# A Mamba block with a ternary feed-forward layer: both layer norms from one set of statistics, small operations moved to GpSimd, weight quantised before the loop, 80 instead of 88 C products on GpSimd

## The reference

```
def mamba_dir(h, ...):                      # once forward, once on the flipped sequence
    x, z = h @ W_in.T                       # 256 channels each
    x = silu(conv4(x) + conv_b)
    dt, Bm, Cm = x @ Wx.T                   # 64 + 16 + 16
    dt = softplus(dt @ Wdt.T + bdt)
    hc = exp(dt * A) * hc + dt * x * Bm     # over 1024 steps, 256 channels x 16 states
    y  = sum_n(hc * Cm) + x * D
    return (y * silu(z)) @ W_out.T
def layernorm(x): return (x - mean(x)) / sqrt(var(x) + 1e-5)

x  = layernorm(h + mamba_fwd(h) + flip(mamba_rev(flip(h))))
# feed-forward
xn = (x - mean(x)) * rsqrt(var(x) + 1e-3) * ln_gamma + ln_beta
w_q = clip(round(w / (mean|w| + 1e-5)), -1, 1);  gamma = max|xn| over everything
y  = clip(xn * 128 / gamma) @ w_q * (gamma * mean|w| / 128)
out = layernorm(x + y)
```

## Time and profile before

| | |
|---|---|
| time, three runs | 985.17, 985.58, 991.32 us (median 985.58) |
| the profiled execution | 983.27 us, of which the span of the core is 981.4 us |
| granted TensorE clock, mean | 0.819 of full speed |
| DVE busy | 883.9 us, 90% of the span, 998 instructions |
| POOL busy | 860.1 us, 88%, 392 instructions |
| ACT / PE busy | 594.0 us, 61% / 647.7 us, 66% |
| the loop | about 42 to 928 us; before it the set-up, behind it the tail |

### The profile page before, as it was taken

One profiled execution on the slowest core, in us unless ns is written; L12 is line 12 of the kernel. 1 busy time (PEld: TensorE's weight loads), 2 busy tenths in 40 slices (PEclk: granted clock), 3 DMA queues, 4 the chain that ended last, 5 costly groups with the idle time before them and its releaser, 6 DMA issues. The chain is left out here.

```text
span 981.4 us, 8254 instructions
## 1 busy us (share of the span) xinstructions
PE 647.7 (66%) x2076; PEld 216.6 (22%) x2076; DVE 883.9 (90%) x998; ACT 594.0 (61%) x966; POOL 860.1 (88%) x392
## 2 busy tenths in 40 slices
PE   6667666868676767858576767757576677655432
PEld 3222122213122222213122121213122121111032
DVE  2388999999999999999999999999999999999945
ACT  2576556665765656665766666665665756663415
POOL 0399999999999999999999999999999999999502
PEclk9977888779798798789699798889699887577656
DMA  2767347564454747564454746564544746640102
GB/s 58 196 174 140 120 86 161 121 133 107 92 141 96 170 86 152 129 135 102 89 144 96 172 86 142 139 129 103 91 123 97 175 86 137 144 87 12 50 26 85
DMA packets 46735, 113.11 MB, mean 115 GB/s; under 512 B 7136, under 2 KB 20448, under 8 KB 46560
## 3 DMA queue, kind: packets, MB, share of 16 engines
q1 hardware_dynamic: 46688, 112.59, 51.4%
HBM read 40.48 MB, written 4.98 MB: 46 GB/s over the span
## 5 line engine op out<-in xcount | busy, mean ns | idle before, releaser
L428 POOL TENSOR_TENSOR dbx<-step_rep,bc_rep 128x1024 f32<-128x1024 f32 x256 | 598.2, 2364 | 16.7 <-DMA step_rep<-step 12.0
L623 ACT ACTIVATE da_ps<-step_rep,neg_a 128x512 f32<-128x512 f32 x512 | 349.7, 689 | 276.0 <-DVE hs L882 270.4
L882 DVE TENSOR_TENSOR_SCAN hs<-da_ps,dbx 128x512 f32<-128x512 f32 x256 | 297.1, 1210 | 30.2 <-POOL dbx L428 14.4
L882 DVE TENSOR_TENSOR_SCAN hs<-da_ps,carry,dbx 128x512 f32<-128x512 f32 x256 | 312.9, 1270 | 12.2 <-ACT da_ps L623 11.8
L1131 PE MATMUL y_ps<-ch,stack 128*32 128x512 f32 x1024 | 173.5, 755 | 188.4 <-DVE ch L770 121.3
L438 POOL TENSOR_TENSOR ch<-hs,bc_rep 128x1024 f32<-128x1024 f32 x88 | 207.7, 2361 | 27.5 <-issue 16.6
L770 DVE TENSOR_TENSOR ch<-hs,c_ps 128x1024 f32<-128x1024 f32 x168 | 201.4, 1199 | 0.0
L1122 PE MATMUL c_ps<-x_dbl,select 128*128 128x512 f32 x256 | 175.5, 774 | 0.0
L1077 PE MATMUL pre<-h_t,w_conv 128*128 128x512 f32 x256 | 119.4, 610 | 6.9 <-ACT xs L529 5.4
L1131 PEld LDWEIGHTS y_ps<-ch,stack 128*32 128x32 f32 x1024 | 24.4, 119 | 300.4 <-issue 173.8
L1122 PEld LDWEIGHTS c_ps<-x_dbl,select 128*128 128x128 f32 x256 | 46.2, 225 | 140.6 <-issue 127.7
(11 more groups left out here) (127 smaller groups left out, 500.5 us busy)
## 6 DMA issues: line engine op xcount, KB each, us to landing
step_rep<-step SPq DMA_DIRECT2D x128, 512.0 KB, 8.3
bc_rep<-bc_rows SPq DMA_DIRECT2D x64, 512.0 KB, 5.6
h_in<-in_L_attn_hidden_states SPq DMA_DIRECT2D x4, 512.0 KB, 8.8
h_res<-in_L_attn_hidden_states SPq DMA_DIRECT2D x4, 512.0 KB, 9.1
out<-hs SPq DMA_DIRECT2D x4, 512.0 KB, 3.2
x_rows<-xn SPq DMA_DIRECT2D x7, 256.0 KB, 7.9
dbx<-x_rows SPq DMA_DIRECT2D x1, 1536.0 KB, 6.6
bc_rows<-x_dbl SPq DMA_DIRECT2D x16, 64.0 KB
```

The source lines that it names most:

```text
L428: nc.gpsimd.tensor_tensor(dbx[:, n % RING], dtx_rep[:, r], b_rep[:, s % 2, k, :].unsqueeze(1).to_broadcast([P, 2, CHUNK]), ALU.mult).then_ ...
L623: nc.scalar.activation(da_ps[:, half % DA_BANKS, :], dt_rep[:, r, e, :], ACT.Exp, scale=neg_a[:, half_of(unit), 2 * (unit % 2) + e, g, k:k ...
L882: nc.vector.tensor_tensor_scan(in_scan_order(hs[:, n % RING, e, :], s), in_scan_order(da_ps[:, (2 * n + e) % DA_BANKS, :], s), in_scan_ord ...
```

## The change

Variance under a second layer norm follows from the first: if v is the variance of `resid`, x has variance v/(v+eps1), and the two norms together multiply by (v(1+eps2) + eps1*eps2) ** -0.5. So both come from one mean and one variance.

- DVE keeps `resid`, four `bn_stats` and four `bn_aggr` (into `mv`). The second set of statistics, both additions of eps and both biases leave DVE.
- POOL gets `both_norms` at n = 6 in place of `inverse_deviation` at n = 6 and at n = 9: three small `tensor_scalar` (128x4), one power of 128x8, one product 128x8, with a wait on its own result ahead of the last two.
- ACT at n = 8: `normalise`, now `resid` -> `xhat`, a new tile that PE transposes; at n = 9: `keep_x1`, `resid` -> `xn`, with the other scale. In the tail `keep_x1` comes after `norm_out`.
- `residual` on DVE waits until ACT has read the `resid` before (`xn_ready`, `x1_ready`), not for PE.
- `quantise_weight` moves into `copy_weights`, after the first copy, ahead of a wait for PE.
- `POOL_C` has five units in every group, (1, 4, 8, 11, 13): 80 C products on POOL, 176 on DVE.

```
-CLOSING = {"save": 3, "start sum": 3, "gate": 2, "output": 4, "residual": 5, "mean1": 6, "deviation1": 6,
-           "bias1": 7, "scale1": 8, "statistics2": 8, "mean2": 9, "deviation2": 9, 
-           "bias2": 10, "scale2": 11, "transpose": 12, "affine": 14, "largest": 14}
+CLOSING = {"save": 3, "start sum": 3, "gate": 2, "output": 4, "residual": 5, "mean": 6, "deviation": 6,
+           "scale": 8, "keep": 9, "transpose": 12, "affine": 14, "largest": 14}
-POOL_C = ((1, 3, 6, 8, 11, 13), (1, 4, 8, 11, 13)) * (NG // 2)
+POOL_C = ((1, 4, 8, 11, 13),) * NG
...
-            def inverse_deviation(e, mv, mv_ready, rstd, rstd_ready, eps):
-
-                pool.wait_ge(mv_ready, 2 * (e + 1))
-                nc.gpsimd.tensor_tensor(rstd[:], mv[:, :, 1], half[:, 0:TT], ALU.pow).then_inc(rstd_ready, 1)
+            def both_norms(e):
+
+                pool.wait_ge(mv_ready, e + 1)
+                if e:
+                    pool.wait_ge(x1_ready, TT * e)
+                    pool.wait_ge(xn_ready, TT * e)
+                nc.gpsimd.tensor_scalar(spread_of[:, 0, :], mv[:, :, 1], LN1_EPS, None, ALU.add).then_inc(spread_ready, 1)
+                nc.gpsimd.tensor_scalar(spread_of[:, 1, :], mv[:, :, 1], 1.0 + LN2_EPS, LN1_EPS * LN2_EPS,
+                                        ALU.mult, ALU.add).then_inc(spread_ready, 1)
+                nc.gpsimd.tensor_scalar(neg_mean[:], mv[:, :, 0], -1.0, None, ALU.mult).then_inc(spread_ready, 1)
+                pool.wait_ge(spread_ready, 3 * (e + 1))
+                nc.gpsimd.tensor_tensor(rstd[:].rearrange("p l t -> p (l t)"), spread_of[:].rearrange("p l t -> p (l t)"),
+                                        half[:, 0:2 * TT], ALU.pow).then_inc(rstd_ready, 1)
+                pool.wait_ge(rstd_ready, e + 1)
+                nc.gpsimd.tensor_tensor(bias[:], rstd[:], neg_mean[:].unsqueeze(1).to_broadcast([P, 2, TT]),
+                                        ALU.mult).then_inc(bias_ready, 1)
...
             def normalise(b_e, h_e):
                 e = 2 * b_e + h_e
-                act.wait_ge(bias1_ready, e + 1)
+                act.wait_ge(bias_ready, e + 1)
+                if e:
+                    act.wait_ge(xn_ps, e)
+                for j in range(TT):
+                    nc.scalar.activation(xhat[:, j, :], resid[:, j, :], ACT.Identity, scale=rstd[:, 1, j:j + 1],
+                                         bias=bias[:, 1, j:j + 1]).then_inc(xn_ready, 1)
+            def keep_x1(b_e, h_e):
...
+                    nc.scalar.activation(xn[:, j, :], resid[:, j, :], ACT.Identity, scale=rstd[:, 0, j:j + 1],
+                                         bias=bias[:, 0, j:j + 1]).then_inc(x1_ready, 1)
...
             def copy_weights():
                 dve.wait_ge(weights_ps, 1)
                 nc.vector.tensor_copy(w_z_t[:], c_ps[:, 0, 0:INNER]).then_inc(weights_sb, 1)
+                quantise_weight()
                 dve.wait_ge(weights_ps, 4)
...
+            def residual(b, h_e):
...
+                dve.wait_ge(o_ps, e + 1)
+                if e:
+                    dve.wait_ge(xn_ready, TT * e)
+                    dve.wait_ge(x1_ready, TT * e)
...
+            def mean(b, h_e):
+
+                e = 2 * b + h_e
+                dve.wait_ge(stats_ready, TT * (e + 1))
+                if e:
+                    dve.wait_ge(bias_ready, e)
                 for j in range(TT):
                     ins = nc.vector.bn_aggr(mv[:, j, :], stats[:, j, :])
                 ins.then_inc(mv_ready, 1)
...
-                        if first and s == 1 and n == 4:
-                            quantise_weight()
```

More of the change, by code:

```diff
@@ L164, in build @@
         stats = sb("stats", [P, TT, 6])
[L165 to L170, removed]
+        mv = sb("mv", [P, TT, 2])
+        spread_of = sb("spread_of", [P, 2, TT])
+        neg_mean = sb("neg_mean", [P, TT])
+        rstd = sb("rstd", [P, 2, TT])
+        bias = sb("bias", [P, 2, TT])
+        xhat = sb("xhat", [P, TT, P])
         xn = sb("xn", [P, TT, P])
@@ L469, in batch @@
                             e = 2 * b if s else 2 * b - 1
[L470 to L473, removed]
+                            if n == CLOSING["deviation"]:
+                                both_norms(e)
             pool.wait_ge(w_sum, 1)
@@ L480, in _ @@
             batches(pool, batch)
[L481 to L483 removed]
+            both_norms(2 * BATCH - 1)
             pool.wait_ge(max_ready, 2 * BATCH + 1)
@@ L680, in _ @@
             normalise(BATCH - 1, 1)
-            normalise_again(BATCH - 1, 1)
             norm_out(BATCH - 1, 1)
+            keep_x1(BATCH - 1, 1)
             per = TILES // BATCH
@@ L795, in aggregate @@
                 ins.then_inc(mv_ready, 1)
[L797 to L838, removed]
             def largest(b, h_e):
@@ L854, in batch @@
                     for n in range(UNITS):
[L855 to L860, removed]
                         for e in range(2):
@@ L885, in batch @@
                                                          initial, ALU.mult, ALU.add).then_inc(scanned, 1)
-                        if s == NG - 1:
-                            norm_first(b, 0, n)
-                        if s == 0 and not first:
-                            norm_first(b - 1, 1, n)
+                        closing = (b, 0) if s == NG - 1 else (b - 1, 1) if s == 0 and not first else None
+                        if closing and n == CLOSING["residual"]:
+                            residual(*closing)
+                        if closing and n == CLOSING["mean"]:
+                            mean(*closing)
                         if n:
@@ L900, in batch @@
                             gate(b - 1, 3)
-                        if s == NG - 1:
-                            norm_second(b, 0, n)
-                        if s == 0 and not first:
-                            norm_second(b - 1, 1, n)
+                        if closing and n == CLOSING["residual"]:
+                            statistics(*closing)
                         if n == CLOSING["largest"] and s == 3:
@@ L920, in _ @@
             gate(BATCH - 1, 3)
-            for n in range(UNITS):
-                for layer in range(2):
-                    if n == CLOSING[f"mean{layer + 1}"]:
-                        statistics_wait(2 * BATCH - 1, layer)
-                norm_first(BATCH - 1, 1, n)
-                norm_second(BATCH - 1, 1, n)
+            residual(BATCH - 1, 1)
+            statistics(BATCH - 1, 1)
+            mean(BATCH - 1, 1)
             largest(BATCH - 1, 1)
@@ L963, in last_sum @@
                     last = j == 2 * BATCH - 2
-                    if not last:
+                    if last:
+                        dve.wait_ge(x1_ready, TT * 2 * BATCH)
+                    else:
                         dve.wait_ge(x1_in, 16 * 2)
```

57 lines of the change are left out of this document (26 added, 31 removed).

## The result

The changed kernel takes 945.73 us (median of four runs, 942.61 to 947.11) against 986.31 of the kernel before on the same chips: ratio 0.9575, 95% interval 0.9534 to 0.9616. That is 40.6 us less; 31 were forecast, as 955, and the range of 943 to 968 held it. The profiled execution has a span of 940.8 us after 981.4.

The account below looks back on a forecast made before the run. DVE was taken to bound A, B and C, and POOL to bound D. The terms sum to 30.9 us less: 983.3 profiled gives 952.4, plus 2.3 for the median 954.7, said as 955; range 943 to 968.

Parts of the forecast that it names:

- A, three: Stretch of group 3's end and group 0's start: 57.2 to 54.6, POOL the limit; 2.6 less, three times, 7.8.
- B, three: Stretch of the rest of group 0: falls to 54.4 with POOL's load; 3.4 less, three times, 10.2.
- C, four: Stretch in groups 1 to 3 that DVE set before: neither load changes, stays 53.0; nothing gained.
- first B: First batch's B, 56.4 us: without the quantisation it is a C stretch of 53.0; 3.4 less.
- D three, last D and A: Stretch of groups 1 to 3 that POOL set: 0.4 less, four times, 1.6; last A: 4.5 less.
- tail's closing: Tail from 939.10 to 946.80: 7.7 us now, 4.3 after; 3.4 less.
- The price of `both_norms`: New POOL work in each closing: small operations at 0.2, power 1.65, two waits of 0.17; 2.8 us, from 2.2 to 6.7.
- The rivals that rested on its price: `both_norms` on POOL dearer: at 5 us 970, at 4 us 963, chance 0.15; near 6 no change, 976, 0.06.
- the slower one: `both_norms` at 8.6 us makes the kernel 1% slower, each small operation 1.6 us or more: 996, chance 0.03.
- The allowance: A and B after the change: 0.5 us added for places where POOL still waits, giving 54.6 and 54.4.
- ACT's waits come back: A and B: DVE waits for ACT's exponentials again when closings are short; 1 us more, six times, 961; chance 0.17.
- The rival of the better balance: D falls to POOL's 51.0 + 0.5 and C with it by 1: 10 less, 945; chance 0.17.

Follow-up runs that it names:

- e6: Changed kernel with the power of eight columns done twice on POOL, 1.67 us more in each closing; ratio to before 0.9724, 13.6 us more than the changed kernel.
- e7: Changed kernel with six more bn_stats in each closing on DVE, 1.7 us more; ratio to before 0.9660, 7.3 us more than the changed kernel.
- e8: Changed kernel with three small operations ahead of the power on ACT instead of POOL; ratio to before 0.9581, 0.5 us less than the changed kernel.
- e2: Kernel before with five C products of a group on POOL everywhere, nothing else; ratio to before 0.9980, 2.0 us less, not told from none.
- e9: Changed kernel with four kinds of small DVE operation on unread 128x4 tiles, without semaphores, in groups 1 and 2; 983.0 us in its one run.
- e1: Kernel before with the weight's quantisation moved into the set-up, nothing else; ratio to before 0.9953, 4.6 us less.
- e10: Changed kernel with POOL's five C products at units 1, 3, 8, 11, 14; ratio to before 0.9494, median 935.28 us.
- e3: Kernel before with only the joint layer norms, 88 C products on POOL and quantisation in the loop; ratio to before 0.9686, 31.0 us less.
- e4: Changed kernel with 88 C products on POOL as before, so norms and quantisation only; ratio to before 0.9649, 34.7 us less.

## Why the prediction was right, and where it was off

The terms of the sum, forecast and as the step products of both profiled executions give them:

| term | forecast | measured |
|---|---|---|
| A, three | 7.8 | 9.7 |
| B, three | 10.2 | 12.1 |
| C, four | 0 | 6.1 |
| first B | 3.4 | 5.5 |
| D three, last D and A | 6.1 | 4.2 |
| tail's closing | 3.4 | 3.1 |
| sum, before rounding | 30.9 | 40.6 of the span's 40.6 |

- *What bounds each stretch.* DVE in A, B and C, POOL in D before; POOL in A and B after. e6, e7 and e8 show the latter, for A with DVE close behind. For the kernel before e2 agrees in the main: 8 products off POOL were worth 2.0 us, not told from none, while DVE set A, B and C. But DVE got a product more in B, and A and B together did not grow.
- *The price of `both_norms`.* 2.8 taken, 2.85 to 2.91 measured. The choice near the lower end, by the small slope of the plain product, held. That the sum came out so closely is partly luck: two waits of 0.17 were taken, and four gaps of 0.08 came. The rivals that rested on its price fall, the slower one too.
- *The small operations of DVE.* 5.2 us a closing was taken; e9 shows the cause given as plausible, a wait for a POOL instruction to end.
- *The allowance.* I added 0.5 us to A and B on top of 54.1 and 53.8; they came at 53.9 and 53.9. POOL's idle time there is 0.4 us, and the gaps inside `both_norms`, already in the 2.8, are most of it. The A and B terms were mis-sized by 1.9 each over three stretches, most of it that allowance (1.5 and 1.8).
- *The step that failed* is "C: neither load changes: 53.0, nothing". The load of a stretch before was not the load of a group: DVE came into it behind and was busy 50.3 us, 1.8 more than in the C of the changed kernel (32.4 scans and 11.5 products, where a group has 32 and 11). With its 2.7 us of waits that was the whole stretch; the prediction added 4.3, of which 1.6 lie ahead of the cut. The first batch's C stands behind the quantisation in the same way, 52.5 then and 50.9 in e1 and after. I had used this very row, C at 53.0, as the measure of an undisturbed stretch for the first B too, which is why that term was 2 us short: 3.2 us came from the quantisation (e1, where POOL is then busy for all of the 53.2) and 2.3 from the product that left POOL.
- *D.* 0.4 each was forecast, 0.2 came. The load argument was right: DVE's 51.35 us and 1.7 of waits for ACT are the whole stretch, and in e10 it fell by 2.1 when two products stood elsewhere.
- *Last D and A.* 0.4 and 4.5 were forecast, 3.5 came. DVE lost 3.8 us of busy time there, as the product that it gets in the last D takes 1.2 of the closing's 5.2, and 0.8 us of waits for ACT came back.
- *ACT's waits come back.* DVE waited 25.1 us for ACT before and 32.1 after. As a rival this was given 961 by way of A and B. In A the waits stayed at 0.6. Of the 7 us some 3.3 lie in the B stretches, where POOL sets the time, as the text against it said; the rest is in C, D and the last stretch, where DVE sets much of the time. The rival of the better balance had the sum nearly right (945) for a wrong reason: it saw D and C fall by the balance of the products, and it was C that fell, by the norms (e3, e4).

## What to carry to other kernels

When two engines are coupled by a ring, cut the trace at an event that both pass, and count the units of each engine in each stretch before using its length as a load: a stretch in which an engine runs more than its share is paying a debt from elsewhere. Count by busy time over the mean of one, as a window's own count and its list of waits take in what merely reaches over the cut. Taking work off the engine that is not the limit may be worth nothing alone and a good deal after the other part of the change (here 2 us, not told from none, and about 7), so cost the parts in that order. Where an engine must wait for another's table change, give it an independent piece of work at that place; moving two products in each group by one unit was worth 9 us here, about as much as the eight products moved off POOL.

## What the hardware showed beyond that

- Beside a POOL that runs product after product, a DVE `tensor_tensor` or `scalar_tensor_tensor` with two SBUF inputs of 128x4 takes 1.4 to 1.6 us and gets in between two POOL instructions (e9, 16 of 16); a `tensor_scalar` from SBUF to SBUF takes 1.55 to 6.6 us, half of them past two such boundaries. A `tensor_reduce` of 128x4 takes 0.14 us there, and `bn_stats` of 128x128 and `bn_aggr` take 0.28 and 0.15 in the changed kernel's loop: they do not wait. POOL's small `tensor_scalar` takes 0.19 to 0.26 us.
- The set-up varies by up to 5 us between profiles of kernels with nearly the same set-up: the first step product on POOL starts at 28.68 us in the changed kernel's profile and at 33.37 in e1's. The windows of 9 to 16 us and of 20 to 35, changed kernel and then e1:

```profile
9.00:16.00 7.00, 6.02 (x15) 2.58 (x16) 2.22 (x9) 0.70 (x2) 0.41 (x1) 1.00 0.25 22
...
20.00:35.00 15.00, 12.67 (x40) 6.09 (x40) 4.75 (x17) 7.44 (x9) 2.35 (x1) 1.00 0.39 95
...
9.00:16.00 7.00, 6.19 (x10) 2.51 (x10) 2.42 (x9) 0.65 (x2) 0.40 (x1) 1.00 0.25 22
...
20.00:35.00 15.00, 12.47 (x41) 6.49 (x40) 2.59 (x6) 8.82 (x10) 1.63 (x1) 0.77 0.21 74
```

In the first window PE has 15 matmuls in the one and 10 in the other, with a granted clock of 1.00 in both, and e1 lost 2.1 us by it; the rows do not show why, and it stays open. The rest was lost from 20 us on, where the granted clock was 0.77 in e1 and 1.00 in the changed kernel. Between the two profiles of the changed kernel itself, 2.0 of 6.2 us are such set-up time (28.68 and 30.66). Single profiles should be compared from the first step product on.
